# A gated recurrence: reset and update gate as two tanh of ScalarE with scale and bias operands, in place of one fused step of VectorE and one tanh

## What is computed

```python
def step(h, x_t):
    hid = jnp.broadcast_to(h[:, None, :], (Bn, Sn, Hn))
    combined = jnp.concatenate([hid, enc_hiddens], axis=2)
    score = jnp.tanh(jnp.einsum('bsk,kh->bsh', combined, W_att))
    score = jnp.einsum('bsh,h->bs', score, V_att[:, 0])
    attn = jax.nn.softmax(score, axis=-1)
    context = jnp.einsum('bs,bsh->bh', attn, enc_hiddens)
    inp = jnp.concatenate([x_t, context], axis=1)
    gz, gr, gh = jnp.split(inp @ Wi + b, 3, axis=1)
    rz, rr, rh = jnp.split(h @ Uh, 3, axis=1)
    z = jax.nn.sigmoid(gz + rz)
    r = jax.nn.sigmoid(gr + rr)
    hh = jnp.tanh(gh + r * rh)
    h_new = z * h + (1.0 - z) * hh
    return (h_new, h_new)
```

## Time and profile before

| | |
|---|---|
| median of 3 runs | 4724.21 us (4721.77 to 4732.26) |
| the profiled execution | 4725.9 us, of which its span 4724.1 us |
| recurrence, first to last `update` | 328.7 to 2352.5 us of the span |
| busy over the span | PE 88%, DVE 61%, ACT 49%, POOL 19% |

### The profile page before, as it was taken

How to read it: one execution, slowest core, us unless ns; L and a number is a source line. 1 busy time by engine, 2 the same in 40 slices (tenths; PEclk the granted TensorE clock), 3 DMA queues, 4 the chain that set the end, 5 groups by cost and what they waited for, 6 DMA issues and landing times. The chain is left out here.

```text
span 4724.1 us, 82263 instructions
## 1 busy us (share of the span) xinstructions
PE 4135.0 (88%) x25322; PEld 2378.3 (50%) x25322; DVE 2861.7 (61%) x13564; ACT 2329.2 (49%) x6588; POOL 913.8 (19%) x4350
## 2 busy tenths in 40 slices
PE   6789999999999999999898999678888888888788
PEld 2247777777777777777732334222333323333223
DVE  4546666666666666666654444546666667666323
ACT  3335655555565556565533334224555544455433
POOL 0123333333333333333231000200011000000002
PEclk8889999999999999999999999768888888888889
DMA  0000000000000000000001000011112111211000
GB/s 9 24 7 2 2 2 2 2 2 2 2 2 2 2 2 2 2 2 2 20 16 46 0 1 1 29 59 43 53 46 64 54 60 52 64 45 44 14 17 5
DMA packets 48983, 94.51 MB, mean 20 GB/s; under 512 B 11440, under 2 KB 31936, under 8 KB 48288
## 3 DMA queue, kind: packets, MB, share of 16 engines
q1 hardware_dynamic: 48544, 89.24, 5.9%
HBM read 72.89 MB, written 15.39 MB: 19 GB/s over the span
## 5 line engine op out<-in xcount | busy, mean ns | idle before, releaser
L761 PE MATMUL ps<-g_h,w_p 128*128 128x128 f32 x4096 | 918.6, 306 | 0.0
L2138 ACT ACTIVATE t_ex<-ps 128x1024 f32<-128x1024 f32 (+1 forms) x480 | 471.9, 1021 | 570.8 <-PE ps L2085 557.1
L761 PEld LDWEIGHTS ps<-g_h,w_p 128*128 128x128 f32 x4096 | 618.0, 191 | 0.0
L757 PE MATMUL ps<-g_h,w_p 128*128 128x77 f32 x2048 | 456.7, 304 | 169.7 <-DVE g_h L829 141.0
L2233 DVE TENSOR_REDUCE t_ncol<-ps 128x1 f32<-128x512 f32 x768 | 486.6, 684 | 152.7 <-PE ps L2058 152.2
L825 DVE SCALAR_TENSOR_TENSOR g_used<-g_encg,g_e 128x77 f32<-128x77 f32 x3072 | 550.8, 230 | 0.0
L795 ACT ACTIVATE g_th<-ps 128x77 f32<-128x77 f32 x1024 | 241.4, 236 | 527.5 <-PE ps L757 527.5
L871 POOL TENSOR_SCALAR g_z<-g_tzr 128x1 f32<-128x1 f32 x1024 | 194.9, 190 | 1414.9 <-ACT g_tzr L804 1414.9
L757 PEld LDWEIGHTS ps<-g_h,w_p 128*128 128x128 f32 x2048 | 305.3, 188 | 305.8 <-DVE g_h L829 298.5
L776 PE MATMUL ps<-g_th,g_vrep 128*128 128x77 f32 x2048 | 456.7, 305 | 0.5 <-ACT g_th L795 0.5
L834 DVE TENSOR_REDUCE g_ntop<-ps 128x1 f32<-128x77 f32 x1024 | 244.6, 239 | 337.1 <-PE ps L776 336.3
(11 more groups left out here) (429 smaller groups left out, 6855.9 us busy)
## 6 DMA issues: line engine op xcount, KB each, us to landing
t_qst<-t_turn_q SPq DMA_DIRECT2D x288, 96.0 KB
t_kst<-t_turn_k SPq DMA_DIRECT2D x144, 96.0 KB
t_turn_q<-t_part SPq DMA_DIRECT2D x24, 384.0 KB, 2.5
t_turn_k<-t_part SPq DMA_DIRECT2D x12, 384.0 KB, 3.3
t_wf<-in_t_wf SPq DMA_DIRECT2D x6, 514.5 KB, 5.5
m_experts<-in_experts SPq DMA_DIRECT2D x1, 3072.0 KB, 13.2
t_wa<-in_t_wa SPq DMA_DIRECT2D x6, 448.0 KB, 3.3
t_wx<-in_t_wx SPq DMA_DIRECT2D x6, 448.0 KB, 4.2
```

The source lines that it names most:

```text
L757: M(att[c], w["att_h"], h[t % 2][:, c:c + 1].broadcast_to([P, S]), start=False, stop=True, skip_group_check=True).then_inc(*st.sem("att", c))
L761: return M(G[c][:, g], weights, h[t % 2][:, c:c + 1].broadcast_to([P, P]), start=False, stop=last, skip_group_check=True)
L2138: A(ex[0:kw, slot[pf, c, l, n]], ps[0:kw, at:at + 2], ACT.Exp, scale=SCALE).then_inc(*st.sem(f"{pf}e{n}", c))
```

## The change

Outside the loop, `encg` for the two gates is copied with a factor 0.5 in place of 1, so that the halving for the tanh is in the weighted sums already. In the loop, the fused step `zr` is gone from `mix`. Instead DVE copies the recurrent part of both gates, halved, from PSUM into `zr` (`halve_gates`), ahead of `mix`. ACT then applies tanh to the raw weighted sums: `tr` for the reset gate and `tz` for the update gate, each on one column, with `sinv` as scale operand and a column of `zr` as bias operand. `tr` needs only the first weighted sum, `tz` the second. The candidate waits for `in` and `tr`; POOL's `factors` wait for `tz`.

```diff
-                        V.tensor_copy(encg[:, g, c], ps[:, 4 * c + 1, 0:S]).then_inc(*pre.sem(f"c{g}_s", c))
+                        V.tensor_scalar(encg[:, g, c], ps[:, 4 * c + 1, 0:S], 0.5 if g < 2 else 1.0, None, ALU.mult)\
+                            .then_inc(*pre.sem(f"c{g}_s", c))
...
-        st = Steps(k, "g", 2, pe="att score gates", act="tanh exp tzr cand",
-                   dve="top sinv r z hm zr in h", pool="z1 omz zh saved")
+        st = Steps(k, "g", 2, pe="att score gates", act="tanh exp tr tz cand",
+                   dve="top gs sinv r z hm in h", pool="z1 omz zh saved")
...
                 def candidate(c, t):
-                    act.wait_ge(*st.at("zr", c, t))
-                    A(tzr[:, c], zr[:, c], ACT.Tanh, scale=0.5).then_inc(*st.sem("tzr", c))
+                    act.wait_ge(*st.at("gs", c, t))
+                    act.wait_ge(*st.at("sinv", c, t))
+                    act.wait_ge(*st.at("r", c, t))
+                    A(tzr[:, c, 1:2], mac[:, c, 1:2], ACT.Tanh, bias=zr[:, c, 1:2], scale=sinv[:, c:c + 1]).then_inc(*st.sem("tr", c))
+                    act.wait_ge(*st.at("z", c, t))
+                    A(tzr[:, c, 0:1], mac[:, c, 0:1], ACT.Tanh, bias=zr[:, c, 0:1], scale=sinv[:, c:c + 1]).then_inc(*st.sem("tz", c))
                     act.wait_ge(*st.at("in", c, t))
-                    act.wait_ge(*st.at("tzr", c, t))
+                    act.wait_ge(*st.at("tr", c, t))
...
+                def halve_gates(c, t):
+                    if t:
+                        dve.wait_ge(*st.at("tz", c, t - 1))
+                    dve.wait_ge(*st.at("gates", c, t))
+                    nc.vector.tensor_scalar(zr[:, c], G[c][:, 0:2, 0], 0.5, None, ALU.mult).then_inc(*st.sem("gs", c))
...
                     dve.wait_ge(*st.at("gates", c, t))
-                    dve.wait_ge(*st.at("z", c, t))
-                    fma("zr", c, zr[:, c], mac[:, c, 0:2], sinv[:, c:c + 1], G[c][:, 0:2, 0])
...
                         update(1, t - 1)
+                    halve_gates(0, t)
                     mix(0, t)
                     top(1, t)
                     update(0, t)
+                    halve_gates(1, t)
...
-                    pool.wait_ge(*st.at("tzr", c, t))
+                    pool.wait_ge(*st.at("tz", c, t))
```

## The result

The changed kernel takes 4982.9 us, median of 4 runs (4975.5 to 4989.0), beside 4726.9 us for the kernel before in the same runs: 1.054 of its time, 95% interval 1.052 to 1.056. That is 256 us slower, where 238 were forecast. The profiled execution took 4986.5 us, its span 4984.7. The forecast was 4962 us; the measured median lies 3 us above the 4980 that went with the longest tanh, and well inside the range of 80%.

What follows compares the result with a forecast made beforehand. The lane's own chain bounds now; the circle through ACT's queue takes over, 0.48 + 0.14 + 0.275 + 0.465 + 0.58 + 0.27 = 2.21 us, 0.232 over 1.978, times 1,024 = 238 us: 4962 us, 80% range 4905 to 5035.

Steps and rivals of the forecast that it cites:

- the circle through the other lane's tanh: ACT's queue puts one lane's tanh ahead of the other's gates; this becomes the bound, 2.21 us per half round.
- D: Length of each gate's new one-column tanh from SBUF with two operands on ACT: 375 ns, ends 351 and 384.
- The 0.14 behind the tanh: On ACT, the time from the start of one lane's tanh to the other lane's tr: 0.14 us.
- D - 0.10: On ACT, from tr's start to tz's start, as an instruction lies 0.10 over the next: 0.275 us.
- D + 0.09: From tz's start on ACT to POOL's first factor: 0.465 us.
- 0.58: From POOL's first factor to the update of the state: 0.58 us.
- update to attend: From the state's update to the lane's next attend on PE: 0.27 us.
- 1.46 + 2D: The circle's half round written with the tanh length D: 2.21 us, against 1.978 us per update before.
- A: Rival: the tanh from SBUF are cheap, 0.204 us each, so the kernel gets faster, 4611 us; 6%.
- B: Rival: the lanes settle so the other lane's tanh isn't in the way; the lane's own chain rules, 4775 us; 4%.
- C: Rival: tr follows the other lane's tanh on ACT at 0.20 us, not 0.14: +61 us, 5023 us; 12%.
- D, the clock: Rival: PE's clock falls as PE idles 0.40 us in each half; time above 6300 us; 3%.

Runs made afterwards that it cites:

- The split without operands: The kernel before with its one two-column tanh split into two one-column tanh without operands, reset gate first: 4780.4 us, ratio 1.011.
- the half change: Against the changed kernel, the update gate is back to a fused DVE step and a plain one-column tanh; the reset gate stays as changed: 4772.5 us, ratio 1.011.
- the kernel without operands: The changed kernel with constants as scale and bias in both gates' tanh, so division and recurrent part are missing: 4634.2 us, ratio 0.978.
- the kernel with the gates first: The changed kernel with both gates' tanh moved ahead of the other lane's tanh in ACT's queue, the candidate staying behind it: 5876.4 us, ratio 1.243.
- the filled kernel: The changed kernel plus one matmul per lane step behind open_att whose result nobody reads: 4976.5 us, ratio 1.052.
- the kernel with the shorter POOL part: z*h made in one POOL operation with h/2 as both operands: 5120.7 us in the changed kernel, 4782.0 us in the kernel before.

## Why the prediction was right

The bound. That the circle through the other lane's tanh takes over was right. Swapping two instructions moved the time by 84 us, and shortening the two tanh by 92 ns each moved the half round by 0.18. Moving them out of the circle closed the reverse one. The split without operands and the half change show that the length of the two tanh is the price, and not their number.

The terms. D was put at 375 ns and is 377 and 374. The 0.14 behind the tanh is 0.14; D - 0.10 is 0.27; D + 0.09 is 0.47; 0.58 is 0.58; update to attend is 0.28 where 0.27 stood. The half round is 2.215 undisturbed, for 2.21. One side remark is off: by 1.46 + 2D, a D of 373 ns in place of 375 gives 4 us less in all, not 2; the forecast doesn't use it.

The copy. It was to push the reciprocal back by up to 0.13 us; the reciprocal starts 0.07 behind it (1203.74 to 1203.81). Hidden either way: the run without it has the same undisturbed half round.

The candidate done 0.42 before the update: 0.43 in the trace.

The rivals. A, cheap tanh: they are 377 ns; the kernel without operands shows what A would have been, 4634, where A said 4611. B, the lanes find a phase: the half rounds are alike in both lanes, each at the 2.22 of the circle, so the lanes found no phase free of it. C, 0.20 behind the tanh: 0.14. D, the clock: I gave it 3%, in the form of a steady fall, and took from 80% busy at a full clock in the loop's first 5 us that PE's idle time was safe. That step was too sure, and that it did no harm to the forecast is luck: the share came out at 82% as reckoned, and the clock fell all the same, for stretches of some 7 us in which PE's matmuls are slower; filling the idle time removed it. In the changed kernel it cost about 7 us of the loop; in the kernel with the gates first the fall cost 640 us, with 3.09 us per half round.

The 18 us that the sum lacks (256 for 238): in the profiled execution, 2.215 for 2.21 gives 5, the average of 2.227 for 2.215 another 12, of which the falls of the clock are the 7 that the filled kernel gained and the late updates the rest (16 times 0.35), and 6 lie outside the loop; together 23, for 4986.5 - 4725.9 = 261 less 238. The kernel before has late updates too, which its average of 1.978 holds already; that the near hit needed the falls, the late ones and the part outside the loop to stay small was not foreseen.

No version beat the kernel before with the full computation. Only the one whose tanh had no operands did, and it isn't the same function.

## What to carry to other kernels

Where two chains are interleaved by hand in one queue, work out the circle that passes through both: from one chain's step to the other's through the shared queue and back. It can have slack in every busy share and still become the bound when two instructions on it get longer. An operand that moves arithmetic into an instruction isn't free where latency rules: removing a 217 ns step from DVE was paid with twice 92 ns on each of two ACT instructions, on the one queue where the lanes meet. And a change that makes PE wait may cost a second time through its clock; a kernel with its idle time filled tells the two costs apart.

## What the runs showed of the hardware

An operand read per partition costs about 92 ns on ACT (377, 285 and 194 ns for two, one and none on a one-column tanh); the Trainium skill, in "ScalarE: Activation LUTs", section "What ACT_TABLE_LOAD costs", says about 93, and the trace agrees.

On POOL two such operands took a 0.19 us step to 0.34, and it began 0.09 us later behind its wait (0.18 for 0.09).

An update on DVE, which has such an operand, starts 0.14 us after the ACT instruction that it waits for, where the reciprocal, which has none, starts 0.04 after ACT's accumulator read (1203.68 to 1203.72 in the kernel before). That the operand is the reason is only argued; behind POOL's last step the same update starts after 0.10 (1203.74 to 1203.84 in the kernel with the shorter POOL part).

The granted clock fell from 1.00 to 0.50 in a loop in which PE waits for the state 0.40 us at a time, and now and then 0.8 us: for some 7 us at a time in the changed kernel, and for the rest of the loop in the kernel with the gates first, where PE had waited 0.74 us twice just before. Extra matmuls in the gaps kept it at 1.00 in all three kernels where they were tried. Yet the kernel without the copy, whose PE idles as long in a half round but whose updates are never late, stayed at 1.00 without them; what starts a fall is open.

In the changed kernel every 64th update started about 0.35 us late with its inputs ready, in the one without the copy none did. The cause is open.
